# First stage of a graph-network kernel in another order, with its LayerNorms' reciprocal deviations made by GpSimd

## What is computed

```python
def _layernorm(x, axis=-1, eps=1e-05):
    m = jnp.mean(x, axis=axis, keepdims=True)
    v = jnp.var(x, axis=axis, keepdims=True)
    return (x - m) / jnp.sqrt(v + eps)
...
    h = jnp.maximum(_layernorm(x, axis=-1), 0.0)
...
        z = _ln(x, ln1_g, ln1_b)
...
            q = (z @ Wq + bq).reshape(L, H, D)
            k = (z @ Wk + bk).reshape(L, H, D)
            v = (z @ Wv + bv).reshape(L, H, D)
            scale = 1.0 / jnp.sqrt(jnp.asarray(D, z.dtype))
            scores = jnp.einsum('ehd,ehd->eh', q[row], k[col]) * scale + bias
            m = jax.ops.segment_max(scores, row, num_segments=L)
            p = jnp.exp(scores - m[row])
```

## Time and profile before

| | us |
|---|---|
| median of 3 runs (392.17 to 392.61) | 392.35 |
| the profiled execution, its own time | 392.51 |
| its span | 391.0 |
| PE busy | 371.8 (95%) |
| DVE busy | 312.3 (80%) |
| ACT busy | 171.6 (44%) |
| POOL busy | 4.2 (1%) |

### The profile page before, as it was taken

How to read it: one execution, slowest core, us unless ns; L and a number is a source line. 1 busy time by engine, 2 the same in 40 slices (tenths; PEclk the granted TensorE clock), 3 DMA queues, 4 the chain that set the end, 5 groups by cost and what they waited for, 6 DMA issues and landing times.

```text
span 391.0 us, 5100 instructions
## 1 busy us (share of the span) xinstructions
PE 371.8 (95%) x1782; PEld 280.6 (72%) x1782; DVE 312.3 (80%) x660; ACT 171.6 (44%) x287; POOL 4.2 (1%) x19
## 2 busy tenths in 40 slices
PE   2889999999999999999989999999999999999994
PEld 2545566666657888887768788887578878787883
DVE  5889999999948689897876978499875778488356
ACT  5664665563145233343568623361363531125320
POOL 4000000000000000000000000000000000000000
PEclk9999999999999999999999999999999999999999
DMA  7602444343126000067400321400420032000002
GB/s 234 259 1 70 148 155 148 106 140 121 58 80 218 1 3 0 2 216 268 161 2 1 123 94 31 183 2 0 134 83 0 3 106 108 3 0 0 2 6 101
DMA packets 16360, 32.92 MB, mean 84 GB/s; under 512 B 1360, under 2 KB 1488, under 8 KB 16336
## 3 DMA queue, kind: packets, MB, share of 16 engines
q1 hardware_dynamic: 15744, 32.25, 24.2%
q10 hardware_dynamic: 592, 0.36, 0.4%
HBM read 21.07 MB, written 1.05 MB: 57 GB/s over the span
## 4 chain that ended last, share of the span: by engine, by line
PE 77%; DVE 14%; ACT 4%; issue 3%; DMA 1%; DVEq 0%; ACTq 0%
PE acc L1395 12%; PE bank L1377 10%; PE bank L1480 7%; PE bank L1270 6%; PE bank L1271 6%; PE bank L1251 4%; PE acc L1251 4%; PE acc L1270 4%; PE acc L1271 4%; PE bank L1465 3%; PE acc L1451 3%; DVE big_rounded L651 2%; PE acc L1228 2%; PE bank L1228 2%; PE acc L1545 2%
## 5 line engine op out<-in xcount | busy, mean ns | idle before, releaser
L1395 PE MATMUL acc<-wide_rounded,c_rounded 128*126 128x512 f32 x200 | 59.5, 439 | 0.7 <-ACT acc L463 0.7
L1395 PEld LDWEIGHTS acc<-wide_rounded,c_rounded 128*126 128x126 f32 x200 | 37.0, 187 | 19.7 <-issue 13.0
L791 DVE TENSOR_SCALAR wide_rounded<-iota_f,picked 128x512 fp32r<-128x512 f32 x100 | 42.2, 481 | 1.5 <-issue 1.1
L482 ACT COPY z_sb<-acc 126x512 f32<-126x512 f32 x37 | 21.6, 584 | 42.0 <-PE acc L1395 33.3
L506 ACT ACTIVATE wide<-wide,low_col 128x512 f32<-128x512 f32 x32 | 21.3, 716 | 32.9 <-DVE low_col L904 32.8
L624 DVE TENSOR_TENSOR wslot_rounded<-wslot,wide_rounded 128x512 fp32r<-128x512 f32 x24 | 16.2, 687 | 21.3 <-ACT wslot L376 21.3
L1480 PEld LDWEIGHTS bank<-v_sb,big 128*128 128x128 f32 x256 | 29.7, 192 | 4.7 <-issue 4.3
L1480 PE MATMUL bank<-v_sb,big 128*128 128x65 f32 x256 | 31.6, 278 | 0.0
L797 DVE TENSOR_TENSOR c_rounded<-row_bc,wslot_rounded 128x1008 fp32r<-128x1008 bf16 x25 | 30.0, 1202 | 0.0
L1377 PE MATMUL bank<-t_sb,wslot 128*128 128x512 f32 x64 | 29.5, 594 | 0.5 <-ACT t_sb L458 0.5
L651 DVE TENSOR_TENSOR big_rounded<-big,big_rounded 128x1024 fp32r<-128x1024 f32 x24 | 29.1, 1222 | 0.5
(11 more groups left out here) (310 smaller groups left out, 765.8 us busy)
## 6 DMA issues: line engine op xcount, KB each, us to landing
big<-z_sb SPq DMA_DIRECT2D x36, 252.0 KB
big<-in_w SPq DMA_DIRECT2D x4, 2048.0 KB, 7.7
x_sb<-in_x SPq DMA_DIRECT2D x8, 256.0 KB, 5.1
big<-in_w_3t SPq DMA_DIRECT2D x2, 1024.0 KB, 6.7
row_bc<-in_rows SPq DMA_DIRECT2D x7, 256.0 KB, 6.5
wslot<-in_wq SPq DMA_DIRECT2D x1, 1024.0 KB, 9.1
wslot<-in_wk SPq DMA_DIRECT2D x1, 1024.0 KB, 11.0
wslot<-in_wv SPq DMA_DIRECT2D x1, 1024.0 KB, 13.0
```

The costliest lines, as they stand in the source:

```text
L482: nc.scalar.copy(stage[0:BROWS, b % STAGES, :], a).then_inc(S["staged"], 1)
L791: nc.vector.tensor_scalar(hot_ring[:, u, k, :], iota_f[:, :], picked[:, 0, s0 + k:s0 + k + 1], None, ALU.is_equal)
L1395: last = nc.tensor.matmul(to, st_ring[:, u, 2 * k + a, :, :].rearrange("p w k -> p (w k)"), hot_ring[:, u, k, :], start=False, stop=False, ...
```

## The change

SP waits until the last tile of x has landed before it issues the loads of the Q, K and V weights. On POOL, a column of -0.5 is set at the start, and for each of the two LayerNorms POOL adds epsilon to the four variances and raises the sums to the power of -0.5, as soon as all four are there; `ln_stds` on ACT, its load of the square root's table, and the reciprocals on DVE are gone. DVE takes the moments of x's tile 3 ahead of `slot_picks`, makes the first coefficients before the slot columns, and takes the moments of h ahead of the first two one-hots. Two of the four `z_turned` go from ACT to DVE, and stand there ahead of the weights of the first slots, the other two one-hots of group 0 and its left sides. Seven steps of Q stand on PE ahead of the pairs of group 0, and the list is one group ahead from there: 7 before group 0, 4 after it, 2 after each of groups 1 to 11, 1 after each of the next eleven.

```diff
-        qkv_group = [g for g, steps in enumerate([7, 4, 3] + [2] * 10 + [1] * 10 + [0]) for _ in range(steps)]
+        qkv_group = [g for g, steps in enumerate([7, 4, 2] + [2] * 10 + [1] * 11 + [0], -1) for _ in range(steps)]
...
+            sp.wait_ge(S[f"x_in{NT - 1}"], 16)
...
+            nc.gpsimd.memset(half_c[:, :], -0.5).then_inc(S["pool_order"], 1)
...
+            for n in range(2):
+                pool.wait_ge(S["ln_var"], n * NT + NT)
+                nc.gpsimd.tensor_single_scalar(std[:, :], mv[:, :, 1], LN_EPS, ALU.add).then_inc(S["pool_order"], 1)
+                pool.wait_ge(S["pool_order"], 4 + n)
+                nc.gpsimd.tensor_tensor(rstd[:, :], std[:, :], half_c[:, 0:1].broadcast_to([P, NT]), ALU.pow
+                                        ).then_inc(S["ln_std"], NT)
...
-            nc.scalar.activation(std[:, 0:1], eps_c[:, :], ACT.Sqrt).then_inc(S["scalar_order"], 1)
-            act.wait_ge(S["scalar_order"], 2)
-            ln_stds(0)
...
-            ln_stds(1)
...
-            z_turned(2)
-            z_turned(3)
...
-                link(nc.vector.reciprocal(rstd[:, :], std[:, :]))
...
+            def z_turned(t):
+
+                dve.wait_ge(S["turned"], t + 1)
+                nc.vector.tensor_scalar(t_sb[:, t, :], bank[Z_BANKS[t]][:, :], colp("ln1_g", t), colp("ln1_b", t),
+                                        ALU.mult, ALU.add).then_inc(S["t_vector"], 1)
+
...
             x_moments(2)
+            x_moments(3)
             slot_picks(0, 0, whole)
-            x_moments(3)
+            ln_coefs(0)
             slot_columns(0, 0, whole)
-            ln_coefs(0)
             step(3, slot_masks(early), False)
+            for t in range(NT):
+                dve.wait_ge(S["h_ready"], t + 1)
+                moments(t, h_sb, "ln_var")
             dve.wait_ge(S["tables"], 7 + NT)
             one_hots(0, 0, (0, 1))
-            for t in range(NT):
-                dve.wait_ge(S["h_ready"], t + 1)
-                moments(t, h_sb, "ln_var")
-            slot_weights(3, early)
-            one_hots(0, 0, (2, 3))
             ln_coefs(1)
             for t in (0, 1):
                 ln_plain(1, t, h_sb)
+            dve.wait_ge(S["cols_in"], 16)
+            for t in (2, 3):
+                z_turned(t)
+            slot_weights(3, early)
+            one_hots(0, 0, (2, 3))
             left_sides(0, 0)
...
-                    if qkv_group[(n + 1) * NT - 1] + RING == g:
+                    if max(qkv_group[(n + 1) * NT - 1], 0) + RING == g:
...
+            pe.wait_ge(S["t_ready"], 2)
+            pe.wait_ge(S["t_vector"], 2)
+            for n, after in enumerate(qkv_group):
+                if after < 0:
+                    qkv_step(n)
             for g in range(NG - 1):
                 pairs(g, g % RING, held[GROUP * (g % 2):GROUP * (g % 2 + 1)])
                 if g == 0:
-                    pe.wait_ge(S["t_ready"], NT)
-                if g == 1:
                     pe.wait_ge(S["weights_read"], 1)
```

More of the change, by code:

```diff
@@ L843, in _ @@
                 moments(t, h_sb, "ln_var")
-            slot_weights(3, early)
-            one_hots(0, 0, (2, 3))
+            dve.wait_ge(S["tables"], 7 + NT)
+            one_hots(0, 0, (0, 1))
             ln_coefs(1)
```

16 lines of the change are left out of this document (5 added, 11 removed).

## The result

The changed kernel takes 394.87 us (median of six runs, 394.82 to 395.22). The kernel before, on the same chip, takes 392.31 (six runs, 392.16 to 392.61). The ratio is 1.0065, with a 95% interval of 1.0052 to 1.0078: **2.6 us slower**. The profiled executions are 394.88 and 392.51 us, with spans of 393.4 and 391.0.

The account below looks back on a forecast made before the run. PE and DVE were both taken to be at their limit in the first stage. DVE's 3.1 us delay, less 1.06 of waits and 0.34 of slack, adds 1.7 us: 394.1 us from the median 392.35, range 392.4 to 395.8.

Parts of the forecast that it names:

- Two engines at their limit, 1.4 us to give: First stage: PE and DVE both full; DVE can absorb 1.06 us of waits plus 0.34 us of lead.
- The slack of 0.34 us: At group 24, DVE hands over its build 0.34 us before PE wants it.
- The dummy matmuls' end at 19.38: On PE, dummy matmuls end at 19.38, so only 0.75 of 1.2 us gained on z reach the transposes.
- The first LayerNorm: POOL's add and power end at about 12.0, hidden before DVE takes h's moments at about 13.85.
- POOL's power at 0.5 us: In each LayerNorm, POOL's add takes 0.3 us and its power 0.5, with a wait of 0.1 each.
- The lock-out: Second LayerNorm: DVE's one-hots block POOL's add, so POOL starts behind both; 394.4 us instead of 394.1.
- Emptying the banks: Ahead of the Q steps: DVE empties two tiles from 21.25 at 0.6 us each, ACT two by 22.55.
- PE's own gain of 0.85 us: Q steps start at 22.6, not 25.36; less group 0's pairs, PE alone gains 0.85 us.
- PE waits about 0.8 us ahead of group 4: First stage: PE, at group 4 by 44.9, waits about 0.8 us for DVE's build, done at 45.7.
- PE decides: Rival: DVE's busy rows hide waits, so DVE catches up and PE's 0.85 us remain; 391.5 us, chance 0.15.
- Partly absorbed: Rival: DVE catches up half its lateness in places not visible; 393.1 us or a little less, chance 0.15.
- POOL is late: Rival: POOL's second pair ends at 18.8 behind the one-hots, transposes 0.35 us later; 394.4 to 396 us, chance 0.20.

Follow-up runs that it names:

- e7: Kernel before with two unread reductions (1.2 us of DVE work) put ahead of group 1's build: 392.5 us against 392.4, ratio 1.0001.
- e8: Kernel before with six unread reductions (3.6 us of DVE work) put ahead of group 1's build: 394.54 us against 392.4, ratio 1.0054.
- e1_fill: Changed kernel with the first slots' weights and group 0's last two one-hots ahead of DVE's two z_turned: 393.86 us, kernel before 392.57.
- e4: Changed kernel with four staging tiles for finished blocks instead of three: 395.04 us, kernel before 392.57.
- e9: Changed kernel with each of the first four Q steps waiting only for its own t_sb tile, transposes' banks exchanged: 395.12 us, kernel before 392.5.
- e2: As e1_fill, with group 0's left sides also ahead of DVE's two z_turned: 394.33 us, kernel before 392.57.
- e3: Changed kernel with all four z_turned back on ACT, Q steps still ahead of group 0's pairs: 394.54 us, kernel before 392.57.
- e5: Kernel before with only the new list, seven Q steps ahead of group 0's pairs: 397.62 us against 392.4, ratio 1.012.
- e12: e6 plus Q steps waiting tile by tile and PE's block numbers loaded one group earlier: 391.17 us, kernel before 392.5.
- e11: Kernel before with only SP's wait for x's last tile ahead of the weights' loads: 392.52 us against 392.5, ratio 1.0001.
- e6: Kernel before with POOL's powers and DVE's new LayerNorm order, four one-hots ahead of the shifts; old list, z_turned on ACT: 391.83 us against 392.4.
- e10: Kernel before with only POOL's powers replacing ACT's roots and DVE's reciprocals, old order: 394.08 us against 392.5, ratio 1.0031.

## Why the prediction was right, and where it was off

The forecast was 394.1 us with a range of 392.4 to 395.8, and slower at 0.72. The result, 394.87, has the forecast's sign and, for the changed kernel, its mechanism, and is 0.8 us above it, just outside the 393.5 to 394.8 that the prediction gave its own case. By the steps:

**Two engines at their limit, 1.4 us to give: right.** e7 and e8 show it without the rest of the change, 0.85 and 0.95 us absorbed ahead of the row. For the changed kernel and e1_fill, e4 and e9 the start's shift less the row's is 1.02 to 1.05 us; for e2, e3 and e5, with the 0.21 us by which their ring-bound one-hots are longer, it is 1.03 to 1.04. The prediction said 1.06.

**The slack of 0.34 us: 0.21 was had.** Against the row's 2.58 the profiled execution is 2.37 longer. In e7 and e8, with the old list, it is 0.40 and 0.42, with the new list 0.08 to 0.34. Executions of one kernel differ by 0.4 us, so single ones don't tell such differences well. The pairs of groups 23 and 24, which stood at 104.50, stand at

```profile
107.19 3.88 PE acc L1400 x16
```

and thus are 2.69 us later, more than DVE's row. The gap between DVE's hand-over and PE's need of group 24 was not there for the taking at every group: group 22's pairs start at 104.22, about 1 us behind its left sides (done by 103.3, both after), with 0.10 us of idle time ahead of them, and 0.29 ahead of group 18's at 93.01, that the profile calls issue. PE reads the block numbers of two groups into registers ahead of each even group, and in e12, which does that one group earlier, no such idle time is recorded. I take it for the cause, but no run has that edit alone. The 0.2 us that were regained lie behind 123 us, and no run singles them out.

**The loads at nothing: right** (e11).

**The dummy matmuls' end at 19.38: wrong for this execution.** They ended at 16.15 + 1.89 = 18.04, and so the transposes waited 1.47 us for z. It is not the change that made them shorter: e1, e2, e3 and e4 have the same instructions ahead of them, and took 1.89, 1.92, 1.89 and 2.98 us, and the kernel before 2.77, all at a granted clock of 1.00. The forecast read one execution's length as the kernel's. Why it varies no run settles.

**The first LayerNorm: right.** POOL's first pair ended at 12.26 and the moments of h began at 13.56, for 12.0 and 13.85.

**POOL's power at 0.5 us: half of what it took.** It took 1.06 us in the second LayerNorm and the add 0.37 for 0.3. Though the moments of h ended 0.2 us earlier than forecast (16.85), z started at 18.82 and not at 18.3. Since the dummy matmuls were no cap, the whole 0.64 us of z's gain reached the transposes, 19.51 for the forecast's 19.4. Two errors that nearly cancel.

**The lock-out, a rival's mechanism.** On POOL an add that took 0.23 us beside small instructions of DVE took 0.37 beside its one-hots (16.94, while they ran from 16.77 to 17.6), and a power took 1.04 in the first LayerNorm, 1.06 in the second and 1.32 beside two more one-hots (e6). POOL was slowed by 0.02 to 0.28 us, and DVE's one-hots were not (0.85 us for two, for 0.88 in the kernel before). The Trainium skill (SBUF — State Buffer, Who interferes with whom) says that of DVE in a two-port mode and GpSimd whichever issues first has the shared ports for its whole instruction, and the other is blocked. That is one instruction; that POOL would start behind both one-hots, at 17.6, was my reading of it. That reading is refuted: the add was done at 17.31, and the power began at 17.45. The rule itself is not. In e6 the power ended at 18.83, 0.04 us behind the last one-hot, as it would if its last step had to wait for that. No run takes this apart.

**Emptying the banks: the term that was mis-sized most.** DVE began at 21.45 and not 21.25, and took 1.44 us for two tiles (21.45 to 22.89) and not 1.2. I had taken the 0.6 of a tile of V; the 0.75 of L816, which I had as the upper bound, was the nearer row. Weights and one-hots took the 1.11 forecast. That makes the left sides start at 24.00 and not 23.5, and DVE's lateness **3.62 us and not 3.1**. Of the difference 0.07 is rounding: 21.25 + 1.2 + 1.1 is 23.55, and 23.55 - 20.38 is 3.17.

**PE's own gain of 0.85 us: too large.** The Q steps, forecast for 22.6, waited for DVE's second tile until 23.08. That leaves 25.36 - 23.08 - 1.87 = 0.41 us. Nothing in the end hangs on it, since DVE is the later.

The sum with the measured terms is 3.62 - 1.04 - 0.21 = 2.37, which is the difference of the two profiled executions; the forecast's was 3.1 - 1.06 - 0.34 = 1.7. Of the 0.67 between them 0.52 are DVE's lateness and 0.15 the rest.

**"PE waits about 0.8 us ahead of group 4": half right.** In the changed kernel PE waits 0.72 us for ACT in group 3 and 0.73 ahead of group 4. The first hid most of a wait for DVE that e4 shows at 1.11 us. The prediction called itself wrong "if PE has no wait on DVE in this stage", and by the label the changed kernel's profile has none; that DVE holds PE there is shown by e1, e4 and e9, not by that profile.

**What the prediction missed is the ring.** It held the delay of group 0's pairs, from 21.85 to 28.8, against PE only, "PE doesn't need group 0 before 28.9, so nothing is late yet". But it is DVE that needs them, since group 2's build reuses their places. The floor of 29.83 lies 2.17 us above the old start. The number came out since DVE's own lateness was larger than the floor, so the forecast survived a hole in its reasoning. It would have failed on e3. There DVE's own start, with the load of the rounds, would be 27.46 + 1.06 = 28.52, 0.86 us later than before, which the same argument absorbs; the ring made it 30.81, and +1.97 was measured.

**The rivals.** PE decides: refuted by e1 and e9 for this kernel, in which a build still takes 2.7 us, and true of e10 and e12, where PE is the later or DVE waits for it. Partly absorbed: no more was absorbed than counted. POOL is late: its 394.4 is nearer to the result than the forecast, but not for its reason, since the transposes started only 0.1 us later than forecast.

## What to carry to other kernels

Work that is moved ahead of a consumer's first group also delays the moment at which that group's buffers come free. Check a reordering against the producer's need of the ring as well as against the consumer's need of data; here it put a floor 2.17 us above the old start. Where two engines are both full, find by how much each may be late (two delay runs gave 1.2 to 1.4 us where I had worked out 1.4) before moving work from one to the other: a gain on the engine that isn't late is worth nothing (PE's in e9), and a gain on the one that the other waits for is worth those waits (PE's in e12). And if a step must wait for another engine, put independent work ahead of it in the queue: that alone was worth 1.1 us of the 2.6.

## What the runs showed of the hardware

GpSimd took 1.04 us for a power of 128x4 and 0.23 for an add of the same size, and up to 1.32 and 0.37 beside VectorE's one-hots; VectorE's reciprocal took 0.17.

The other surprise was TensorE's clock. A stretch of e10_powers_only (columns as above):

```profile
20.00:24.50 4.50, 3.42 (x17) 3.45 (x18) 4.13 (x9) 1.98 (x3) 0.08 (x1) 0.64 0.00 0
```

The granted clock was 1.00 in this stretch of the kernel before. In e10, behind an idle time of 2.06 us, it read 0.64, with the transposes at half rate, that is at 1.2 GHz; in e5, behind one of 3.27 us, 0.69 from 25 to 29. In the changed kernel it read 1.00 behind idle times of 1.47 and 1.63 us. But it also read 1.00 behind idle times of 2.15 us in e2 and 2.61 us in e3, longer than e10's, so the length of one idle time does not settle it, and no run says what does. An idle time of TensorE may cost more than itself, 1.69 us on top in e5. The runs of e5 lie 1.6 us apart (three and one) and those of e10 about 1.0 (four and two), so a median of few runs says little of a kernel with such an idle time.
